# A decoder layer on one core: next input transposed one slot iteration sooner, u in other PSUM banks, another start for the first batch

## The reference, cut to what matters

```
xn = layer_norm(x);  u, z = split(xn @ W_in.T)             # 512 + 512 columns
u  = silu(causal_conv(u, 4 taps) + b)
dt_in, B, C = split(u @ W_x.T);  dt = softplus(dt_in @ W_dt.T + dt_bias)
h_t = exp(dt*A) * h_(t-1) + dt*B*u ;  y = sum_n h*C + u*D  # 512 channels x 16 states, scan over 512 tokens
x1 = layer_norm(x + (y * silu(z)) @ W_out.T)
slots = x1; repeat 3 times: q from rmsnorm(slots), softmax over slots, renormalised over ctx rows, GRU cell
x2 = layer_norm(x1 + slots);  f = relu(x2 @ W_fc.T)^2 @ W_pr.T
out = layer_norm(x2 + spike_count(f) / 5)                   # 5 steps of a leaky integrator
```

## Times and profile before

| | us |
|---|---|
| median of 3 runs (lowest, highest) | 1699.95 (1696.39, 1705.75) |
| the profiled execution, its own time | 1699.65 |
| its span, first to last instruction | 1697.8 |
| TensorE busy (matmuls) | 1360.2, 80% |
| VectorE busy | 1310.5, 77% |
| ScalarE busy | 989.2, 58% |
| GpSimd busy | 866.1, 51% |
| mean granted TensorE clock | 0.898 of full |

### The profile page before, as it was taken

How to read it: one execution, slowest core, us unless ns; L and a number is a source line. 1 busy time by engine, 2 the same in 40 slices (tenths; PEclk the granted TensorE clock), 3 DMA queues, 4 the chain that set the end, 5 groups by cost and what they waited for, 6 DMA issues and landing times. The chain is left out here.

```text
span 1697.8 us, 16460 instructions
## 1 busy us (share of the span) xinstructions
PE 1360.2 (80%) x5536; PEld 808.5 (48%) x5536; DVE 1310.5 (77%) x1508; ACT 989.2 (58%) x1547; POOL 866.1 (51%) x432
## 2 busy tenths in 40 slices
PE   4465787787888789887888789887888789887787
PEld 1244444454445445454445455454445455453354
DVE  2899688876887898968987888968987888973335
ACT  3644575537665576737765567737765567734522
POOL 0566257644666266644766267644766267640100
PEclk9775898797999899997999989997999989999898
DMA  4733343306332443306332343306331343300000
GB/s 165 262 134 114 140 148 112 111 25 226 123 105 70 140 161 104 118 15 225 128 115 66 128 159 111 119 17 225 126 115 68 125 162 111 116 19 2 12 0 25
DMA packets 64875, 188.96 MB, mean 111 GB/s; under 512 B 6304, under 2 KB 22560, under 8 KB 64832
## 3 DMA queue, kind: packets, MB, share of 16 engines
q1 hardware_dynamic: 64832, 188.43, 32.1%
HBM read 183.62 MB, written 4.78 MB: 111 GB/s over the span
## 5 line engine op out<-in xcount | busy, mean ns | idle before, releaser
L492 POOL TENSOR_TENSOR reg_a<-reg_a,cb 128x1024 f32<-128x1024 f32 (+1 forms) x256 | 600.5, 2355 | 308.3 <-DVE reg_a L1393 302.8
L1393 DVE TENSOR_TENSOR_SCAN reg_a<-reg_a,pb 128x1024 f32<-128x1024 f32 x256 | 584.8, 2284 | 27.3 <-ACT reg_a L1129 15.5
L1129 ACT ACTIVATE reg_a<-dt,neg_a 128x511 f32<-128x511 f32 x512 | 334.6, 710 | 54.1 <-DVE reg_a L1393 53.6
L769 PE MATMUL py<-ident,reg_a 128*128 128x128 f32 x1984 | 286.7, 296 | 83.3 <-POOL reg_a L492 83.3
L1384 DVE TENSOR_TENSOR pb<-bb,pb 128x1024 f32<-128x1024 f32 x256 | 314.5, 1228 | 24.4 <-DVE reg_a L1393 2.9
L769 PEld LDWEIGHTS py<-ident,reg_a 128*128 128x128 f32 x1984 | 250.3, 153 | 172.7 <-POOL reg_a L492 113.8
L630 PE MATMUL px<-hT,whh 128*128 128x512 f32 x252 | 120.2, 604 | 0.0
L457 POOL TENSOR_TENSOR xs<-xs,hT 128x1024 f32<-128x1024 f32 x24 | 56.5, 2354 | 111.5 <-ACT xs L1049 111.5
L734 PE MATMUL pc<-x2T,w_fc 128*128 128x512 f32 x192 | 99.4, 643 | 8.2 <-ACT reg_m L1056 8.2
L742 PE MATMUL pc<-w_pr,reg_m 128*128 128x256 f32 x384 | 90.9, 382 | 8.6 <-ACT reg_m L1058 8.6
L742 PEld LDWEIGHTS pc<-w_pr,reg_m 128*128 128x128 f32 x384 | 69.6, 190 | 25.7 <-ACT reg_m L1056 13.4
(11 more groups left out here) (255 smaller groups left out, 2337.1 us busy)
## 6 DMA issues: line engine op xcount, KB each, us to landing
bb<-bc_rows SPq DMA_DIRECT2D x256, 512.0 KB, 3.6
cb<-bc_rows SPq DMA_DIRECT2D x64, 512.0 KB, 6.3
xin<-x_in SPq DMA_DIRECT2D x9, 512.0 KB, 3.3
xs<-x_in SPq DMA_DIRECT2D x8, 512.0 KB, 3.3
x_out<-reg_m SPq DMA_DIRECT2D x5, 512.0 KB, 3.4
w_in<-w_inT_in SPq DMA_DIRECT2D x1, 1024.0 KB, 6.8
w_fc<-w_fcT_in SPq DMA_DIRECT2D x1, 1024.0 KB, 10.9
w_pr<-w_prT_in SPq DMA_DIRECT2D x1, 1024.0 KB, 13.1
```

The source lines that it names most:

```text
L492: pool.tensor_tensor(h[:, g % HR, 0:n], h[:, g % HR, 0:n], cb[:, 2 * q:2 * q + n], ALU.mult).then_inc(s["hc_done"], 1)
L769: mm = pe.matmul(py[:, cols_], h[:, g % HR, j, cols_], ident[:], is_transpose=True, start=(q == 0 and j == 0 and i2 == 0), stop=(q == PAIR ...
L1129: ins = act.activation(d_a[:, g % DR, j, 1:], dt[:, c, 1:], ACT.Exp, scale=neg_a[:, c * NS + n + j:c * NS + n + j + 1])
L1393: dve.tensor_tensor_scan(h2[:, g % HR], d_a2[:, g % DR], pb[:, 1:3, :].rearrange("p a t -> p (a t)"), 0.0, ALU.mult, ALU.add).then_inc(s[" ...
```

## The change

- The next input is normalised and transposed in the second slot iteration's place (positions 9 to 20) and not in the third's (22 to 29). ACT and DVE lists follow; TensorE's third `norm` waits for the copies (`xnT_ready`), since both use `px` and `st`.
- The chunks of u lie in pb3, pc, px0 and px1. Chunks 0 and 1 are projected before `final`, chunks 2 and 3 right after it (position 32), none waits for the conv. Chunk 3's accumulator is the free half of the tile `silu` (`u_acc`), because `u2[:, 3]` is still read. The x projection goes into `py`, chunk by chunk between the out projections.
- On DVE `final` (the statistics of x2) goes from position 30, ahead of scan 31, to position 33, behind the first conv; the conv is cut into steps by tap.
- Table loads of ScalarE are placed by hand: Silu's at position 31, the Ln/Exp set behind the copy of B and C and no longer at the start of a body.
- Smaller moves: `sp_ln` one position sooner on ACT, ahead of `weigh`; `up` of positions 9 to 11 one later on ACT; spike 5 from the head to behind scan 0; `gate_x` 1 ahead of `down` 0 1 at position 15; `down` 1 1 from position 25 to 24 on DVE.
- Ahead of body 0: own semaphores for `cols` and `w_in`, a wait for each at its first use, transposes that wait tile by tile, and 36 multiplications of the identity by itself on TensorE before them.

```diff
-        u_banks = (px[:, 0, :], px[:, 1, :], pb[:, 3, :], px[:, 0, :])
+        u_banks = (pb[:, 3, :], pc[:], px[:, 0, :], px[:, 1, :])
+        def u_acc(c):
+            return u2[:, c] if c < DT - 1 else uth[:, 0]
...
-        loads = [(cols, cols_d), (w_in, k_rows(w_inT)), (w_x, k_rows(w_xT)), (w_dt, w_dtT)]
+        loads = [(w_x, k_rows(w_xT)), (w_dt, w_dtT)]
+        WARM = 36
...
         at("pe",
-                      (15, ("down", 0, 1), ("gate_x", 1, 0), ("gate_x", 1, 1), ("gate_h", 1, 2)),
-                      (16, ("down", 0, 2), ("gate_h", 1, 3), ("gate_x", 1, 2), ("gate_x", 1, 3)),
-                      (20, ("up", 1, 0), ("up", 1, 1)), (21, ("norm", 2), ("gate_h", 2, 0)),
-                      (29, ("cand_x", 2, 1), ("turn",)),
-                      (30, ("final", 0), ("u", 0), ("u", 1)), (32, ("outp", 0)), (34, ("outp", 1), ("u", 2)),
-                      ("end", ("u", 3), ("outp", 2), ("outp", 3), ("xp",)))
+                      (15, ("gate_x", 1, 0), ("down", 0, 1), ("gate_x", 1, 1), ("gate_h", 1, 2), ("gate_h", 1, 3)),
+                      (16, ("down", 0, 2), ("gate_x", 1, 2), ("gate_x", 1, 3)),
+                      (20, ("up", 1, 0), ("up", 1, 1), ("turn",)), (21, ("norm", 2), ("gate_h", 2, 0)),
+                      (29, ("cand_x", 2, 1)), (30, ("u", 0), ("u", 1), ("final", 0)),
+                      (32, ("u", 2), ("u", 3), ("outp", 0)), (33, ("outp", 1)), (34, ("outp", 2), ("xp", 0), ("xp", 1)),
+                      ("end", ("outp", 3), ("xp", 2), ("xp", 3)))
         at("act",
-                      (1, ("sp_exp",), ("x2t", 0)), (2, ("weigh", 0), ("sp_ln",), ("x2t", 1)),
-                      (9, ("up", 0, 0)), (10, ("sq", 1), ("norm", 1), ("up", 0, 1)), (11, ("up", 0, 2)), (12, ("up", 0, 3)),
-                      (20, ("up", 1, 1), ("sq", 2), ("norm", 2)),
-                      (26, ("gate_x", 2, 0), ("gate_x", 2, 1), ("reset", 2), ("next_norm",)),
-                      (29, ("cand", 2), ("turn",)), (30, ("final", 0)), (31, ("u", 0), ("u", 1)),
-                      (33, ("silu", 0), ("silu", 1), ("u", 2), ("u", 3)), ("end", ("silu", 2), ("silu", 3)))
+                      (1, ("sp_exp",), ("x2t", 0), ("sp_ln",)), (2, ("weigh", 0), ("x2t", 1)),
+                      (10, ("up", 0, 0), ("sq", 1), ("norm", 1)), (11, ("up", 0, 1)), (12, ("up", 0, 2), ("up", 0, 3)),
+                      (18, ("next_norm",)), (20, ("turn",), ("up", 1, 1), ("sq", 2), ("norm", 2)),
+                      (26, ("gate_x", 2, 0), ("gate_x", 2, 1), ("reset", 2)),
+                      (29, ("cand", 2)), (30, ("u", 0), ("u", 1), ("final", 0)), (31, ("u", 2), ("u", 3), ("gate_table",)),
+                      (33, ("silu", 0), ("silu", 1)), ("end", ("silu", 2), ("silu", 3)))
         at("dve",
-                      ("start", ("spike", 0), ("spike", 1), ("spike", 2)), ("head", ("ctx", 0), ("ctx_norm",), ("spike", 3), ("spike", 4), ("spike", 5)),
-                      (23, ("score", 2), ("next_stats",), ("soft", 2)), (24, ("recol", 2)), (25, ("down", 1, 1)),
-                      (("mid", 26), ("next_shift",)), (30, ("final", 0)), (("mid", 32), ("conv", 0)), ("end", ("final", 1), ("conv", 2)))
+                      ("start", ("ctx", 0), ("spike", 0), ("spike", 1), ("spike", 2), ("ctx_norm",)), ("head", ("spike", 3), ("spike", 4)),
+                      (("mid", 0), ("spike", 5)), (10, ("next_stats",)), (("mid", 11), ("next_shift",)),
+                      (23, ("score", 2), ("soft", 2)), (24, ("recol", 2), ("down", 1, 1)), (("mid", 32), ("conv", 0, 0)),
+                      (32, ("conv", 0, 1)), (("mid", 33), ("conv", 0, 2)), (33, ("final", 0), ("conv", 2, 0), ("conv", 2, 1), ("conv", 2, 2)),
+                      ("end", ("final", 1)))
-        at("pool", (22, ("next_stats",)), (30, ("final", 1)))
+        at("pool", (9, ("next_stats",)), (31, ("final", 1)))
...
             pe.wait_ge(consts_done, 6)
-            next_transposes()
-            pe.wait_ge(weights_in, 16 * len(loads))
+            for _ in range(WARM):
+                pe.matmul(pb[:, 0, 0:P], ident[:], ident[:], start=True, stop=True)
+            for i2 in range(TT):
+                pe.wait_ge(s["next_norm"], i2 + 1)
+                ...
+            pe.wait_ge(w_in_in, 16)
             for c in range(DT):
                 u_proj(c)
-            x_proj()
+            pe.wait_ge(weights_in, 16 * len(loads))
+            for c in range(DT):
+                x_proj(c)
...
+                    if mamba and k == TURN + 1:
+                        pe.wait_ge(s["xnT_ready"], ET)
...
             def keep_bc():
                 act.wait_ge(s["xproj_full"], 1)
-                act.activation(xp, px[:, 1, :], ACT.Copy).then_inc(s["bc_kept"], 1)
+                act.activation(xp, py[:], ACT.Copy).then_inc(s["bc_kept"], 1)
+                act.preload_act_table_set(LN_EXP)
```

More of the change, by code:

```diff
@@ L72 @@
 LN_EXP = "natural_log_exp_and_others"
+SILU = "silu_and_others"
+TURN = 1
 COLS = {}
@@ L312, in decoder_layer @@
-                      (19, ("cand", 1), ("up", 1, 0)), (20, ("up", 1, 1), ("sq", 2), ("norm", 2)), (22, ("up", 1, 2)), (23, ("up", 1, 3)),
-                      (24, ("weigh", 2), ("keep_x2",)), (26, ("gate_x", 2, 0), ("gate_x", 2, 1), ("reset", 2), ("next_norm",)),
-                      (27, ("gate_x", 2, 2), ("gate_x", 2, 3)), (28, ("keep", 2)), (29, ("cand", 2), ("turn",)), (30, ("final", 0)),
-                      (31, ("u", 0), ("u", 1)), (33, ("silu", 0), ("silu", 1), ("u", 2), ("u", 3)), ("end", ("silu", 2), ("silu", 3)))
@@ L316, in decoder_layer @@
-        at("dve", ("start", ("spike", 0), ("spike", 1), ("spike", 2)), ("head", ("ctx", 0), ("ctx_norm",), ("spike", 3), ("spike", 4), ("spike", 5)),
-                      (1, ("score", 0)), (("mid", 3), ("soft", 0)), (3, ("recol", 0)), (("mid", 4), ("zed", 0)), (4, ("out_stats",), ("renorm", 0)),
-                      (5, ("zed", 1)), (("mid", 6), ("out_shift",)), (7, ("zed", 2), ("hold", 0)), (8, ("zed", 3)), (13, ("score", 1)),
-                      (("mid", 14), ("soft", 1)), (14, ("recol", 1), ("renorm", 1)), (("mid", 18), ("hold", 1)),
-                      (23, ("score", 2), ("next_stats",), ("soft", 2)), (24, ("recol", 2)), (("mid", 25), ("renorm", 2)), (25, ("down", 1, 1)),
-                      (("mid", 26), ("next_shift",)), (("mid", 28), ("hold", 2)), (28, ("down", 1, 3)), (30, ("final", 0)), (("mid", 32), ("conv", 0)),
-                      ("end", ("final", 1), ("conv", 2)))
+                      (8, ("out_norm",), ("zed", 3), ("cand", 0)), (10, ("up", 0, 0), ("sq", 1), ("norm", 1)), (11, ("up", 0, 1)),
@@ new lines, in decoder_layer @@
+                      (12, ("up", 0, 2), ("up", 0, 3)), (13, ("weigh", 1)), (15, ("gate_x", 1, 0), ("down", 0, 1)),
+                      (16, ("gate_x", 1, 1), ("reset", 1), ("gate_x", 1, 2), ("gate_x", 1, 3), ("keep", 1)), (17, ("down", 0, 3)), (18, ("next_norm",)),
+                      (19, ("cand", 1), ("up", 1, 0)), (20, ("turn",), ("up", 1, 1), ("sq", 2), ("norm", 2)), (22, ("up", 1, 2)), (23, ("up", 1, 3)),
+                      (24, ("weigh", 2), ("keep_x2",)), (26, ("gate_x", 2, 0), ("gate_x", 2, 1), ("reset", 2)), (27, ("gate_x", 2, 2), ("gate_x", 2, 3)),
@@ new lines, in decoder_layer @@
+                      (28, ("keep", 2)), (29, ("cand", 2)), (30, ("u", 0), ("u", 1), ("final", 0)), (31, ("u", 2), ("u", 3), ("gate_table",)),
+                      (33, ("silu", 0), ("silu", 1)), ("end", ("silu", 2), ("silu", 3)))
+        at("dve", ("start", ("ctx", 0), ("spike", 0), ("spike", 1), ("spike", 2), ("ctx_norm",)), ("head", ("spike", 3), ("spike", 4)),
+                      (("mid", 0), ("spike", 5)), (1, ("score", 0)), (("mid", 3), ("soft", 0)), (3, ("recol", 0)), (("mid", 4), ("zed", 0)),
+                      (4, ("out_stats",), ("renorm", 0)), (5, ("zed", 1)), (("mid", 6), ("out_shift",)), (7, ("zed", 2), ("hold", 0)), (8, ("zed", 3)),
+                      (10, ("next_stats",)), (("mid", 11), ("next_shift",)), (13, ("score", 1)), (("mid", 14), ("soft", 1)),
+                      (14, ("recol", 1), ("renorm", 1)), (("mid", 18), ("hold", 1)), (23, ("score", 2), ("soft", 2)), (24, ("recol", 2), ("down", 1, 1)),
+                      (("mid", 25), ("renorm", 2)), (("mid", 28), ("hold", 2)), (28, ("down", 1, 3)), (("mid", 32), ("conv", 0, 0)),
+                      (32, ("conv", 0, 1)), (("mid", 33), ("conv", 0, 2)), (33, ("final", 0), ("conv", 2, 0), ("conv", 2, 1), ("conv", 2, 2)),
+                      ("end", ("final", 1)))
@@ L323, in decoder_layer @@
         at("pool", ("start", ("ctx", 0), ("spike", 0)), (3, ("dt", 1), ("dt", 2), ("dt", 3)), (5, ("out_stats",)), (6, ("keep", 0)), (8, ("cand", 0)),
-                      (17, ("keep", 1)), (18, ("cand", 1)), (22, ("next_stats",)), (28, ("keep", 2), ("cand", 2)), (30, ("final", 1)))
+                      (9, ("next_stats",)), (17, ("keep", 1)), (18, ("cand", 1)), (28, ("keep", 2), ("cand", 2)), (31, ("final", 1)))
```

(7 more changed lines are left out.)

101 lines of the change are left out of this document (55 added, 46 removed).

## The result

The change takes 0.7% off: 1693.07 us (median of 14 runs, 1672.27 to 1694.9) against 1700.57 (14 runs beside them, 1695.92 to 1708.6), ratio 0.993 with a 95% interval of 0.9909 to 0.995. The forecast was 1664. The sign was right, the size a fifth of what was expected.

A forecast was written before the change was run, and what follows sets the result against it. No engine was full, so the waits ending last in each stage were taken as the bound. Start -7.4, body 0 -1, tails -38.5, middles +10.5, drain +0.5: -35.9 from 1699.65, 1664 us; range 1655 to 1672.

The forecast's parts named there:

- Start, -7.4: Ahead of body 0: single load waits and 36 multiplications let B and C leave at 32.9 us against 40.3.
- Rival B: At the start: the clock stays low through the multiplications, start +2.3 in place of -7.4, 1674 us; chance 0.12.
- Tails, -5.5 each: Ends of bodies 1 to 7: u 0 and 1 ahead of a full-pace `final`, norm ending at 1333.2; -38.5 for seven.
- Middle, +1.5 a body: Slot iterations, where work is added: moved steps cost +1.5 a body, +10.5 for seven, range 0 to +3 a body.
- `next_stats` and `next_shift` at position 10: VectorE has no gap there; 2.0 and 0.1 us, partly covered by the 0.99 wait ahead of `soft` 1: +1.1.
- Position 15: Middle of a body: `gate_x` ahead of `down` brings `gate_h` 3 forward, -0.6.
- rival A: `final` stays slow (+1.5 a body) or heads run slow longer (+0.5): +14 on the forecast, 1678 us; chance 0.22.
- The Ln, +0.7: Head of a body: `sp_ln` ahead of `weigh` 0 on the chain, +1.1 less what the head gives back, +0.7.
- `turn`, +0.5: Position 20: transposes free in TensorE's idle time, ScalarE's copies delay the third `norm`: +0.5, at worst +1.5.
- the last -0.2: End of the middle: `next_norm` gone from position 26 and `down` 1 1 one sooner, -0.2.
- Drain, +0.5: Behind the eighth body: same code, but slow first transposes, +0.5.
- Rivals C and D: C: slot chain takes moved work in full, 1726 us, chance 0.05; D: table loads at loop's head, 1677, 0.06.

The follow-up runs named there:

- e6: The changed kernel without the 36 multiplications at the start; 1693.07 us, ratio 0.993 to the kernel before.
- e12: The changed kernel with the next input's statistics at position 14 on VectorE and without the 36 start multiplications; 1666.34 us, ratio 0.9787.
- e19: The changed kernel: statistics at 14, Ln behind `weigh` 0, `next_norm` 26, `turn` 29, 10 multiplications at scan 1, no 36 at start; 1658.02 us.
- e2: The kernel before with the new start alone, the x projection still in one go behind the last Silu; 1693.9 us, ratio 0.998.
- e8: The changed kernel with u 0 and u 1 behind `final` again on TensorE and ScalarE; 1703.16 us, ratio 1.0008.
- shorter kind: Executions of the changed kernel between 1672 and 1687 us, three of 14 runs; the profiled one took 1677.86 us.
- usual kind: Executions of the changed kernel between 1692 and 1695 us, 11 of 14 runs; profiled with 44 start multiplications instead of 36, at 1694.53 us.
- e16: The kernel before with only `next_stats` moved to position 10 (9 on GpSimd) and `next_shift` to 11; 1724.44 us, ratio 1.0146.
- e17: The kernel before with only the Ln of the spikes moved ahead of `weigh` 0; 1706.21 us, ratio 1.0036.
- e9: The changed kernel with 10 identity multiplications between the two half transposes of x2 at scan 1; 1678.9 us, ratio 0.9898.
- e13: The changed kernel with the next input's statistics at position 14 and the Ln behind `weigh` 0; 1666.67 us, ratio 0.9782.
- e7: The changed kernel with statistics at position 14 and 16 identity multiplications at the end of each body; 1665.31 us, ratio 0.9789.
- e3: The changed kernel with 16 more identity multiplications at the end of each body, ahead of the meeting; 1677.01 us, ratio 0.9865.
- e11: The changed kernel with statistics at position 14, Ln behind `weigh` 0 and 10 identity multiplications at scan 1; 1648.91 us, ratio 0.9688.

## Why the prediction was wrong

- **Start, -7.4: right.** Rows out at 32.73, forecast 32.9; the multiplications end at 12.8 and the transposes behind them run at full clock, as forecast. But the 7.4 isn't owed to the multiplications: without them the start is no longer (e6, e12, e19). 3.9 came with the single load waits and the multiplications together (e2); the other 3.7 is where e2 still has the x projection in one go. And the rows' 32.73 is one of two forms, since other executions have 30.1 to 30.5. Rival B (the clock stays low, +2.3) didn't come.
- **Tails, -5.5 each: right.** Measured 5.6, `final` at full clock; e8 shows that u ahead of `final` is the reason for 4.1 of it.
- **Middle, +1.5 a body: the step that failed.** It came to 2.2 in the late bodies of the shorter kind and to 5.6 in those of the usual kind. By its terms:
  - *`next_stats` and `next_shift` at position 10, "+1.1": 1.9.* The prediction counted 2.1 of VectorE less the wait of 0.99 ahead of `soft` 1, and put `next_shift` at 0.1. It takes 1.3 there, because GpSimd's multiply holds it. Alone the move costs 3.5 a body (e16), 1.9 so and 1.6 by the half clock in the third `norm`.
  - *Position 15, "-0.6": +1.3.* The prediction counted `gate_h` 3 as brought forward and not that `down` between the two `gate_x` ends their overlap on TensorE. The runs show the size; the cause is read from the rows.
  - *The clock in the middle, put at nothing.* I looked for its price at `final` and at the head and gave it 2 us a body as rival A. In the usual kind the third `norm` runs at half clock, 1.6 us that the later bodies of before don't have. Behind `soft` 0 the kernel before is slow as well (the earlier trace rows come from a body in which `renorm` 0 is at 38.7); there the shorter kind wins 3.3 us a body, and 3 of 14 executions are of that kind.
- **The Ln, +0.7: right** (e17: 0.9; to `renorm` 0 the usual kind is 0.6 longer). **`turn`, +0.5, and the last -0.2: right** (0.6 at full clock; -0.4).
- **Drain, +0.5: it was 2.0.** VectorE ends the tail, TensorE idles longer, and the first transposes of the drain are slow: before it is 1.09 us for the eight behind 2.31 us of idle time, after

```profile
1506.92 1.96 PE L595 MATMUL px<-ident,x 128*128 128x128 f32 x8 [4.33 <-SPq L431]
```

  That is 0.9; the rest was not followed.
- **Rivals C and D didn't come.** C's mechanism was nevertheless the true one in part: moved work on the chain, priced by it at 10.4 a body and measured at 5.6 in the usual kind. Its turning point of 6.6 a body was missed by one. No table load stands at the loop's head (D).

In the usual kind tails and middles cancel to within 3 us. So the sign of the whole came out right mostly by the start and body 0, and that is in part luck.

What stays open is why one execution has the slow stretch behind `soft` 0 in all late bodies and another has it in none. Kernels with different work come out at equal lengths of late bodies: 191.1 us (before, e2, and the changed kernel in its usual kind), 187.7 (its shorter kind, e9, e13 and e7), 194.6 (e16 and e8). And equal lengths are made differently: at 187.7 the shorter kind is fast behind `soft` 0 (8.5 us to `renorm` 0) and slow in the third `norm`, e13 the other way round (12.1, and the `norm` at full clock). Something pulls bodies to a few lengths, and a saving of 1 us then brings 3.3 or nothing. That it goes through TensorE's clock is shown by e3 and by e11 against e13, which add only idle-time multiplications; what fixes the lengths isn't shown.

## What to carry to other kernels

Ask of each step that is moved into a stretch where an engine has no gap for its whole price there, for a small VectorE instruction with both operands in SBUF what GpSimd runs beside it, and for a step put between two matmuls whether those two ran at once. Where TensorE alternates between its two clocks, a sum of parts gives the sign but not the size: look for the half-clock stretch on the chain and the idle wait in front of it, and try a few multiplications into an idle bank there (18 us here for ten of them in e11 against e13, 14 in e9 against the changed kernel) before reordering real work. Check a kernel's single times, not only the median: here two groups of times were two patterns of the clock. And compare stretch by stretch, each at the same clock, before a difference is put down to a step.
